# A four-stage attention and FFN kernel on one core: loop body in another order, late waits for low parts, fillers on TensorE

## The reference, cut to what matters

```python
# 1 cross attention, 16 heads, 64 keys, and a small MLP behind it
q, k, v = x@Wq+bq, ctx@Wk+bk, ctx@Wv+bv
o = softmax(q k^T / 4) v;   y = relu(o@W1+b1)@W2+b2
# 2 top-2 of 8 experts that share wi and wo and differ by a rank-16 term
inter_e = x@wi.T + bi + (x@A_e.T)@B_e.T;   y = sum_e gate_e * (relu(inter_e)@wo.T + bo)
# 3 cross attention with one head, no scale
y = softmax((x@Wq1+bq1)(ctx@Wk1+bk1)^T) (ctx@Wv1+bv1)
# 4 linear
y = x@weight.T + pooled(x)@disha
```

## Time and profile before

| | |
|---|---|
| median of 3 runs | 358.0 us |
| the profiled execution's own time | 357.66 us |
| its span, first to last instruction | 355.6 us |
| mean granted TensorE clock | 0.98 |
| prologue (to the first `a_scores`) | 0 to 25.4 us |
| body 0, with the setup in it | 25.4 to 58.0 us |
| body 1 | 58.0 to 100.1 us |
| bodies 2 to 6 | 100.1 to 288.3 us, 37.6 us each |
| body 7 | 288.3 to 325.3 us |
| drain and end | 325.3 to 355.6 us |

### The profile page before, as it was taken

How to read it: one execution, slowest core, us unless ns; L and a number is a source line. 1 busy time by engine, 2 the same in 40 slices (tenths; PEclk the granted TensorE clock), 3 DMA queues, 4 the chain that set the end, 5 groups by cost and what they waited for, 6 DMA issues and landing times.

```text
span 355.6 us, 6371 instructions
## 1 busy us (share of the span) xinstructions
PE 314.1 (88%) x2453; PEld 281.2 (79%) x2453; DVE 240.1 (68%) x642; ACT 169.5 (48%) x347; POOL 145.1 (41%) x149
## 2 busy tenths in 40 slices
PE   2456898979989999999999998999899999799992
PEld 2343897769987998699978897889789986799981
DVE  3975478563678667767767766776786676537586
ACT  3135925455445714672565345554456245611711
POOL 2804561615215540636053714462255332441351
PEclk9987999998999999999999999999999999999997
DMA  8389330001300040003200220012000300000000
GB/s 257 100 228 375 106 96 3 2 0 31 89 0 3 12 108 31 0 2 86 65 2 2 61 89 2 0 42 79 31 0 19 74 29 4 0 2 29 2 29 29
DMA packets 14365, 18.83 MB, mean 53 GB/s; under 512 B 2144, under 2 KB 10720, under 8 KB 14080
## 3 DMA queue, kind: packets, MB, share of 16 engines
q1 hardware_dynamic: 12464, 15.12, 15.3%
q10 hardware_dynamic: 1872, 3.31, 2.5%
HBM read 9.51 MB, written 2.62 MB: 34 GB/s over the span
## 4 chain that ended last, share of the span: by engine, by line
PE 57%; DVE 18%; ACT 14%; POOL 5%; DMA 3%; issue 2%; SPq 1%; DVEq 0%; ACTq 0%
PE psI L288 17%; PE psI L428 8%; PE psP L288 8%; PE psS L288 5%; ACT hs L768 3%; PE psT L288 3%; ACT hs_h L773 3%; ACT r L788 3%; PE psP L369 3%; DVE am L1036 2%; PE psS L332 2%; PE psP L370 2%; PE psT L303 2%; PE psS L355 2%; DVE st L975 2%
## 5 line engine op out<-in xcount | busy, mean ns | idle before, releaser
L1359 POOL TENSOR_TENSOR rs<-ve,mhalf 128x2 f32<-128x2 f32 x30 | 21.9, 729 | 121.4 <-DVE ve L984 121.3
L1378 POOL TENSOR_TENSOR hid_l<-r,hid_h 128x512 fp32r<-128x512 f32 x32 | 40.7, 1285 | 19.7 <-ACT hid_h L793 19.7
L788 ACT ACTIVATE r<-psI,first 128x256 f32<-128x256 f32 x60 | 25.0, 476 | 38.4 <-PE psI L428 38.4
L428 PE MATMUL psI<-at_h,lb_h 128*128 128x256 f32 x120 | 36.1, 301 | 5.0 <-ACT r L788 3.9
L1063 DVE SCALAR_TENSOR_TENSOR r<-psI,nbi,r 128x256 f32<-128x256 f32 x60 | 25.5, 476 | 12.6 <-PE psI L428 12.6
L428 PE MATMUL psI<-at_h,lb_l 128*128 128x256 f32 x120 | 33.8, 281 | 0.0
L428 PE MATMUL psI<-at_l,lb_h 128*128 128x256 f32 x120 | 33.7, 281 | 0.0
L1372 POOL TENSOR_TENSOR hs_l<-hs,hs_h 128x512 fp32r<-128x512 f32 x16 | 20.5, 1283 | 30.9 <-ACT hs_h L773 30.0
L1004 DVE RECIPROCAL rec<-psP 128x256 f32<-128x256 f32 x16 | 28.0, 1752 | 5.4 <-PE psP L370 5.4
L428 PEld LDWEIGHTS psI<-at_h,lb_h 128*128 128x128 f32 x120 | 22.6, 188 | 10.2 <-ACT r L788 6.5
L737 ACT ACTIVATE xn<-xmid,nmr,rs 128x256 f32<-128x256 f32 x16 | 8.7, 594 | 44.4 <-POOL nmr L1363 44.4
(11 more groups left out here) (252 smaller groups left out, 890.4 us busy)
## 6 DMA issues: line engine op xcount, KB each, us to landing
stack<-qu_h SPq DMA_DIRECT2D x60, 64.0 KB, 2.0
xin<-in_x SPq DMA_DIRECT2D x8, 256.0 KB, 2.7
stack<-qu_l SPq DMA_DIRECT2D x32, 64.0 KB, 2.0
out<-x ACTq DMA_DIRECT2D x7, 256.0 KB, 2.0
raw_wi<-in_wi SPq DMA_DIRECT2D x1, 1024.0 KB, 6.2
raw_wo<-in_wo SPq DMA_DIRECT2D x1, 1024.0 KB, 9.2
kv<-in_kv SPq DMA_DIRECT2D x2, 384.0 KB, 8.9
raw_w<-in_w ACTq DMA_DIRECT2D x1, 512.0 KB, 6.7
```

Of the source, the lines that this page charges most:

```text
L428: last = mm(bank[:, k * T:(k + 1) * T], (WH, WL)[x]["lb"][:, 0, f * P:(f + 1) * P], AT[y][:, which, :], start=False, stop=q == 2, skip_gro ...
L788: last = A(R1[:, f, :], bank[:, k * T:(k + 1) * T], ACT.Relu, bias=cols[:, BI + f:BI + f + 1])
L1359: G_.tensor_tensor(rs[:, :], ve[:, :], mhalf[:, :], ALU.pow).then_inc(S(f"ln{j}_rs"), 1)
L1378: G_.tensor_tensor(HL[:, two, :], R1[:, two, :], as32(HH[:, two, :]), ALU.subtract).then_inc(S("hidl"), 1)
```

## The change

- New helper `passes`: for several outputs at once it issues one pass after the other. `a_queries`, `a_hidden`, `a_out`, `f_gate` and `f_out` use it and now wait for the high part ahead of the two passes that need only that, and for the low part ahead of the last pass.
- `f_lora_transposes` writes to P_(0), the gate's bank, and `lora_high` and `lora_low` read it there. `c_scores(c, 1)` no longer waits for `at_l`.
- `y` has 320 columns: ScalarE's `linear` copies the scores with it, ahead of `weights_exp`, and `weights_shift` reads them in SBUF.
- TensorE's body is in another order (below), and so are ScalarE's and VectorE's. In VectorE's the statistics of the third layer norm are split: `bn_stats` stands ahead of `experts`, the rest (`moments`) behind `low(3, ...)`. `low(2, ...)` and the residual keep their places.
- `fold_turn` moves from body 1 into body 0, `fold_values` behind `a_queries`. `gw` gets its own memory.
- `filler`: products of a zero tile with itself (float32, 256 columns), 21 in the prologue and 10 in body 0.
- `drain` has `c_scores` and the base and first products in another order, `c_attend` ahead of the four `f_second`, and on VectorE `third_residual` ahead of the four `hidden_sum`.

```diff
+            def passes(parts, chunks, pairs, start, stop):
+                for a, b in pairs:
+                    for i, (out, lhs, rhs) in enumerate(parts):
+                        for k, c in enumerate(chunks):
+                            last = mm(out, lhs(a, c), rhs(b, c), start=start and (a, b) == pairs[0] and i == 0 and k == 0,
+                                      stop=stop and k == len(chunks) - 1, skip_group_check=True)
+                return last
...
             def a_hidden(b, u):
...
+                    pe.wait_ge(S("oh"), (b + 1) * KC)
+                parts = [(S_(u)[:, k * T:(k + 1) * T], w("w1", (2 * u + k) * P), x_of(OA)) for k in range(2)]
+                passes(parts, range(KC), ((0, 0), (1, 0)), True, False)
+                if u == 0:
                     pe.wait_ge(S("ol"), (b + 1) * KC)
-                for k in range(2):
-                    last = three(S_(u)[:, k * T:(k + 1) * T], w("w1", (2 * u + k) * P), x_of(OA), range(KC))
-                last.then_inc(S("hs_ps"), 1)
+                passes(parts, range(KC), ((0, 1),), False, True).then_inc(S("hs_ps"), 1)
...
             def f_lora_transposes(b):
-                    last = nc.tensor.transpose(T_(1)[:, k * P:(k + 1) * P], am[:, k * P:(k + 1) * P], ident)
+                    last = nc.tensor.transpose(P_(0)[:, k * P:(k + 1) * P], am[:, k * P:(k + 1) * P], ident)
...
             def c_scores(b, t):
-                else:
-                    pe.wait_ge(S("atl"), b + 2)
...
+            def filler(bank, count):
+                for _ in range(count):
+                    mm(bank[:, 0:T], zeros[:, 0:P], zeros[:, :], start=True, stop=True)
...
             def body(a, f, c, h):      # TensorE
-                if F_:
-                    f_lora_transposes(f)
                 if A_:
                     a_scores(a, 0)
                     a_scores(a, 1)
+                if F_:
+                    f_lora_transposes(f)
                 if C_:
                     c_scores(c, 0)
                     c_scores(c, 1)
                 if F_:
                     f_first(f, 0)
                     f_first(f, 1)
+                if A_:
+                    a_scores(a, 2)
+                if a == 0:
+                    filler(I_(0), 2)
+                if A_:
+                    a_attend(a, 0)
                 if F_:
                     f_second(f, 0)
                 if f == 0:
-                    fold_turn()
                     fold_means()
-                if A_:
-                    a_scores(a, 2)
                 if C_:
                     c_transpose(c)
                 if F_:
                     f_second(f, 1)
                 if A_:
-                    a_attend(a, 0)
                     a_scores(a, 3)
...
-                if H_:
+                if a == 0:
+                    filler(I_(0), 3)
+                    transposes(1, h, T_(1))
+                    filler(I_(0), 5)
+                if A_:
+                    a_hidden(a, 0)
+                if H_ and a > 0:
...
                     transposes(1, h, T_(1))
                 if A_:
-                    a_hidden(a, 0)
                     a_hidden(a, 1)
                 if H_:
                     a_queries(h)
+                if f == 0:
+                    fold_values()
...
             def body(a, f, c, h):      # ScalarE
                 A_, F_, C_, H_ = (v is not None for v in (a, f, c, h))
+                if A_:
+                    exps(a, 0)
                 if F_:
                     lora_high(f)
                 if A_:
-                    exps(a, 0)
                     exps(a, 1)
-                if F_:
-                    first_relu(f, 0)
-                if C_:
-                    weights_exp(c)
-                    linear(c)
-                if F_:
-                    first_relu(f, 1)
...
+                if C_:
+                    linear(c)
+                    weights_exp(c)
+                if F_:
+                    first_relu(f, 0)
+                    first_relu(f, 1)
...
                 if F_:                 # VectorE, end of the body
                     second_residual(f)
+                    dve.wait_ge(S("x2"), (f + 1) * NT)
+                    statistics(3, f, X2)
                 if A_:
                     experts(a)
                 if F_:
                     low(3, f, XTC, T_(0))
+                    moments(3, f)
                 if A_:
                     gates(a)
-                if F_:
-                    dve.wait_ge(S("x2"), (f + 1) * NT)
-                    norm_stats(3, f, X2)
```

More of the change, by code:

```diff
@@ L384, in a_out @@
                     pe.wait_ge(S("lo_wp"), 1)
+                parts = [(P_(1)[:, t * D:(t + 1) * D], x_of(HS, t * P, P), w("w2", 0, D)) for t in range(NT)]
+                pe.wait_ge(S("hsh"), (b + 1) * NDH)
+                passes(parts, range(NF1), ((0, 0), (0, 1)), True, False)
                 pe.wait_ge(S("hsl"), (b + 1) * NDH)
-                for t in range(NT):
-                    last = three(P_(1)[:, t * D:(t + 1) * D], x_of(HS, t * P, P), w("w2", 0, D), range(NF1))
-                last.then_inc(S("x1_ps"), 1)
+                passes(parts, range(NF1), ((1, 0),), False, True).then_inc(S("x1_ps"), 1)
             def f_gate(b, h):
@@ L393, in f_gate @@
                     pe.wait_ge(S("lo_w"), 4)
-                split_in(2, b)
                 if h is not None:
                     pe.wait_ge(S("ql"), (h + 1) * KC)
-                for t in range(NT):
-                    last = three(P_(0)[:, t * 256:t * 256 + GA], x_of(XTF, t * P, P), w("ga", 0, GA), range(KC))
-                last.then_inc(S("ga_ps"), 1)
+                parts = [(P_(0)[:, t * 256:t * 256 + GA], x_of(XTF, t * P, P), w("ga", 0, GA)) for t in range(NT)]
+                pe.wait_ge(S("ln2_h"), b + 1)
+                passes(parts, range(KC), ((0, 0), (0, 1)), True, False)
+                pe.wait_ge(S("ln2_l"), b + 1)
+                passes(parts, range(KC), ((1, 0),), False, True).then_inc(S("ga_ps"), 1)
             def f_lora_transposes(b):
@@ L442, in f_second, with f_out @@
                 f_lora(b, u, 1, "second_ps", bank)
-            def f_out(b, t, passes=range(3)):
+            def f_out(b, t, high=True, low=True):
                 if t == 0:
@@ L448, in f_out @@
                         pe.wait_ge(S("lo_wp"), 4)
+                    pe.wait_ge(S("hidh"), (b + 1) * NDF)
+                part = [(I_(0)[:, t * D:(t + 1) * D], x_of((HH, HL), t * P, P), w("wo", 0, D))]
+                if high:
+                    passes(part, range(NFF), ((0, 0), (0, 1)), t == 0, False)
+                if low:
                     pe.wait_ge(S("hidl"), (b + 1) * NDF)
-                last = three(I_(0)[:, t * D:(t + 1) * D], x_of((HH, HL), t * P, P), w("wo", 0, D), range(NFF), passes)
-                if t == NT - 1 and 2 in passes:
-                    last.then_inc(S("x2_ps"), 1)
+                    last = passes(part, range(NFF), ((1, 0),), False, True)
+                    if t == NT - 1:
+                        last.then_inc(S("x2_ps"), 1)
             def c_turn(b):
@@ L588, in drain @@
                 c_scores(c, 0)
+                c_scores(c, 1)
                 f_base(f, 2, BANKS[2])
-                c_scores(c, 1)
-                f_base(f, 3, BANKS[3])
                 f_first(f, 0, BANKS[0])
@@ L684, in body @@
                 if F_:
-                    f_out(f, 1, (0,))
+                    f_out(f, 1, low=False)
                 if a == 0:
@@ L694, in body @@
                 if F_:
-                    f_out(f, 1, (1, 2))
+                    f_out(f, 1, high=False)
                 if H_:
@@ L887, in body @@
                     sum_high(f, 1)
+                if A_:
+                    attended(a, 0)
+                if F_:
                     first_relu(f, 2)
+                if A_:
+                    attended(a, 1)
+                if F_:
+                    first_relu(f, 3)
                 if f == 0:
-                    act.wait_ge(S("v1"), 1)
-                    A(VV[0][:, 0:2 * BATCH:2, :], r3(v1, BATCH), ACT.Identity).then_inc(S("vv_h"), 1)
                     act.wait_ge(S("gw"), 1)
                     A(gw_h[:, :], gw[:, :], ACT.Identity).then_inc(S("gw_h"), 1)
-                if A_:
-                    attended(a, 0)
-                    attended(a, 1)
+                if a == 0:
+                    high(1, h, XTA, T_(1))
+                    high_weights("wi")
+                if H_ and a > 0:
+                    high(1, h, XTA, T_(1))
+                if A_:
+                    hidden(a, 0)
+                    hidden_high(a, 0)
+                    hidden(a, 1)
+                if H_:
+                    queries(h)
+                if A_:
+                    hidden_high(a, 1)
                 if f == 0:
@@ L1220, in body @@
                 if F_:
[L1221 to L1225 removed]
+                    hidden_sum(f, 2)
                 if f == 0:
```

130 lines of the change are left out of this document (64 added, 66 removed).

## The result

The changed kernel takes 336.57 us, the median of 4 runs (335.96 to 341.23), against 358.19 for the kernel before in 4 runs beside it (357.07 to 359.44): a recorded ratio of 0.938, 95% interval 0.933 to 0.942. The ratio leaves out the slow one of the four runs, 341.23 us; the two medians as they stand give 0.940. The forecast was 339.4. The profiled execution took 335.96 us with a span of 333.9, 21.7 us shorter than before; the forecast had 18.3.

The account below looks back on a forecast made before the run. TensorE's queue was taken as the bound. Gains of 9.5 (bodies 2 to 6), 5.0 (body 1), 2.0 (prologue, body 0) and 3.6 (body 7), less 1.8 (drain), gave 18.3: 357.7 to 339.4 us, range 334.5 to 346.5.

Parts of the forecast that it names:

- TensorE's queue as the bound, 35.0 us of work in a steady body: Bodies 2 to 6: of 37.6 us, 2.6 are weight-load waits; the other 35.0 is TensorE's own work and the floor.
- The opening, 1.75 us: Start of each steady body: 2.0 us of waits for `at_l` and the relu go, 0.25 of waiting remains.
- Late waits are worth nothing elsewhere in a steady body: Steady bodies: late waits save only 0.2 us, for `hid_l`, since `oa_l` and `xta_l` are there in time before.
- Body 1, 5.0: Body 1: 5.0 us saved, from the wait before the hidden layer, the slow clock, relu waits and `fold_turn`; ends 3.5, 5.8.
- Prologue and body 0, 2.0: Prologue and body 0: 2.0 us saved by fillers holding the clock and an earlier hidden layer; ends +3.8 and -2.
- The first rival: Prologue and body 0: fillers buy nothing, the 2.0 turns into -2, total 343.4 us; chance 0.14.
- the start of the scores is set by the transfers: Prologue: scores begin when the stacked queries' last transfer lands, at 25.0 us, unless the last eight fillers run late.
- Body 7, 3.6: Body 7: 3.6 us saved, 1.8 at the opening, 1.3 at the hidden layer's wait, about 0.5 before the gate.
- Drain, -1.8: Drain: 1.8 us lost, 1.05 at the last product and 0.75 at the opening; ends -0.3 and -3.
- `am` as the new wait: Start of bodies 2 to 7: VectorE's tail costs a microsecond of the opening's gain each, total 345.4 us; chance 0.14.
- the relu held back: ScalarE's first relu waits behind the third stage's exponentials, 3.3 us a body, total 359.2 us; chance 0.02.

Follow-up runs that it names:

- bank_wait: Changed kernel with the low-rank transposes back in T_(1) and `c_scores(c, 1)` waiting for `at_l` again: 345.08 us, ratio 0.961.
- attend_back: Changed kernel with scores and `a_attend(a, 0)` back at their old places among the low-rank products: 343.90 us, ratio 0.956.
- early_waits: Changed kernel with every split product waiting for its low part ahead of its first pass: 355.56 us, ratio 0.995.
- before_late_waits: Kernel before with only `passes` and the late waits for low parts, in the old order: 350.43 us, ratio 0.977.
- no_fillers: Changed kernel with all 31 products of zeros removed: 338.83 us, ratio 0.948.
- trimmed: Changed kernel with the drain's old tail, GpSimd's long operation behind `kd_l`, 14 not 8 fillers before the scores, five not ten in body 0: 332.78 us, ratio 0.924.
- before_pool_late: Kernel before with GpSimd's long operation on the key stack waiting for VectorE's `kd_l`: 356.29 us, ratio 0.990.
- after_pool_late: Changed kernel with GpSimd's long operation on the key stack waiting for VectorE's `kd_l`: 335.33 us, ratio 0.932.
- stats_late: Changed kernel with VectorE's whole third layer norm statistics behind `gates` again: 338.73 us from two runs (335.95, 341.51), no ratio given.
- late_out_only: Changed kernel with low parts awaited up front everywhere but in the MLP's output product `a_out`: 354.10 us, ratio 0.984.
- before_fillers: Kernel before with the 31 fillers alone, at the same places: 355.68 us, ratio 0.987.

## Why the prediction was right, step by step

- **TensorE's queue as the bound, 35.0 us of work in a steady body: right.** It came out at 35.32 with 35.10 busy. That 35.0 is below the 36.04 us of busy time before isn't a contradiction: the forecast took off the waits of weight loads, 2.6 us, and part of these counts as busy time of the matmuls, which stood for only 1.6 (37.62 less 36.04).
- **The opening, 1.75 us: right in mechanism, short in size.** The forecast kept a wait of 0.15 for `xtc_l` and 0.1 for the relu, and 0.05 for the split passes; none shows. `am` came 0.08 behind the body's start, where 0.2 was forecast. The queries' 0.4 was a wait of weight loads; TensorE's matmuls stand only 0.22. bank_wait (0.9) and attend_back (1.24) confirm the two parts: their sum of 2.1 lies close to the 2.0 of waits that the forecast removed.
- **"Late waits are worth nothing elsewhere in a steady body": wrong.** The reason given, that the low parts "are there in time before as well", was read from the old order, where the waits for `at_l` and the relu gave them that time. With these gone, and with early waits, the queue runs into `hs_l`, `hid_l`, `xta_l` and `xtf_l`, for 2.7 us a body. The forecast also didn't price that ScalarE's `queries` now stands ahead of the MLP's second high part, which delays `hs_l` by 1.2 us; how much of the 1.4 at that product comes from it stays open. The total was unharmed because both halves were in the change: the forecast took all waits away, and only its split between the two edits was wrong. By the same reasoning the order alone would have been worth about 15 us (18.3 less 0.15 in each steady body, 1.3 in body 7 and 0.9 in body 0's hidden layer); early_waits is 3 us faster than before, and its steady bodies are slower.
- **Body 1, 5.0: right, 4.9.** Which of its terms gave how much isn't shown singly; before_late_waits gives 2.6 of it without any new order, with its clock at 1.00 in 78.8 to 82.0 as after the change. New small waits are 1.50 for `at_l` at the opening and 0.43 for the residual behind `vv_l`.
- **Prologue and body 0, 2.0: right in sign; 3.25 measured, and from other places.** The forecast had nothing in the prologue and 2.0 in body 0; it came out as 2.4 and 0.86. The first rival is refuted, since zeros lift the clock: the fillers are worth 1.85 in body 0 by no_fillers. It would have been about 3 without the 1.25 of surplus fillers, which the forecast didn't price, and trimmed gets 1.9 back. In the prologue "the start of the scores is set by the transfers" holds, but the transfers follow VectorE's key tiles: GpSimd held up `kd_h` and `kd_l` in the one execution and `kb` in the other. So of the 21.7 up to 2.4 are the luck of two executions: before_pool_late and after_pool_late start their scores within 0.3 us of each other. With the same operation held up the change gains nothing in the prologue: bank_wait and stats_late begin at 26.1, before at 25.4. With `kb` held up it gains 0.9 to 1.1 (22.8 to 23.0 against before_late_waits' 23.92). The profiles speak for the change making the lucky draw likelier, since a `keys0` at the upper clock starts `kd_h` ahead of `xr`; fourteen single executions don't give how often.
- **Body 7, 3.6: near, 3.2.** The wait for `hs_h` is 0.88, 1.34 less than the earlier trace rows; the forecast had 1.3.
- **Drain, -1.8: near, -1.3.** The last product's first pass lost 1.4 of its 3.3 us, as forecast. The 0.7 for `am` and `xtc_l` at its opening is 0.4: TensorE stands 0.2 until `am` ends (302.24, transposes at 302.30) and 0.2 more until `xtc_l` does (302.84, product at 302.90).
- **Rivals.** `am` as the new wait is refuted by the timeline after and by stats_late, the relu held back by the waits after.

## What to carry to other kernels

In a queue that is the bound, a low part or any other late operand "in time" is in time only behind the waits ahead of it: when these are removed, look at every later wait with its slack reduced by what was gained, and try loosening them together, since here one alone handed its time to the next. Look too whether the new order itself makes an operand later, as ScalarE's did here. Products of zeros hold TensorE's clock over a gap, but count them against the gap's length, as every one too many stands on the chain and every one too few lets the clock fall. In setup code look for a VectorE operation whose duration differs between two executions, and for the GpSimd operation beside it and the one ahead of that.

## What the runs showed of the hardware

- VectorE's operations with two inputs in SBUF stood for the time of a GpSimd operation that reads SBUF, and the profile books this as their duration, not as a wait: 0.75 became 4.35, 1.21 became 4.08. In both cases the hold ended 3.5 us behind the recorded start of the GpSimd operation (12.26 - 8.72 and 12.89 - 9.40, each VectorE end less its own work), though that is recorded with 5.37. The Trainium skill's "SBUF — State Buffer", section "Who interferes with whom", says that such a pair shares one read port and that the one that issues second blocks fully; the trace agrees on the block. It goes the other way as well: in late_out_only VectorE's `kb` (10.51 to 11.80) had started first, and GpSimd's operation took 6.14 us instead of 5.37. A VectorE subtraction with one input in PSUM wasn't held: `xta_l` started at 9.43 in after, 0.03 behind GpSimd's operation, and took 0.69 us, as elsewhere.
- Products of a zero tile count for the clock: from 24.1 to 30.8 us it was 1.00 with them and 0.50 without, and it stayed at 1.00 with up to 1.09 us of idle time between the last of them and the scores (early_waits). With 2.99 (after_pool_late) it was 0.50 from 22.0 to 28.0, and with 2.28 (stats_late) 0.68 from 24.1 to 30.8. Behind the same four fillers `keys0`'s eight records took 1.16 to 1.19 us in five profiles, 1.60 to 1.67 in four and 2.02 in one (before_fillers), against 2.04 to 2.08 without: when the clock rises differs from execution to execution.
- The same idle stretch doesn't always lower the clock: TensorE's wait in body 7 of the old kernel was followed by 1.00 in one execution and by 0.56 and 0.60 in two others.
